# A two-layer transformer on one core: the head's set-up work moved between engines, the end of the program cut in parts, and every slot of the software pipeline set anew

## The chip, the cores and the metric

The kernel runs on one core of a Trainium2 chip. The core has five engines that run their own instruction streams and meet only at semaphores: PE (TensorE, matrix products and transposes, results in the eight banks of PSUM), DVE (VectorE), ACT (ScalarE), POOL (GpSimd) and SP (SyncE, which only issues transfers here). The metric is the device time of one execution in microseconds. Three runs of the kernel before gave 383.49, 383.53 and 386.50 us, a median of 383.53 us.

## The reference, cut to what matters

The reference runs two blocks over x with 8 sequences of 256 tokens and 128 features. Each block adds an attention and a feed-forward part to x, each behind a layer norm:

```
x = x + L0_attn(layernorm(x))    # 16 heads of 8, logits - softplus(alpha_h)*|i-j|, softmax
x = x + tanh(h @ W @ A1 @ A2 + bias)          # h = layernorm(x)
x = x + L1_attn(layernorm(x))    # scores * exp(-0.01*|i-j|), softmax; k, v through a rank-32 latent
x = x + L1_ffn(layernorm(x))     # three +-1 matrices 256->512->512->128, relu between
```

So there are 8 sequences x 2 layers = 16 items of 16 heads, each head a softmax over a matrix of 256x256 scores.

## The kernel before, in words

**Tiling and stages.** An item is one sequence in one layer; items 0 to 7 are layer 0, items 8 to 15 layer 1. The main loop has 16 iterations of 16 slots; a slot `s` of iteration `i` brings head `c = 16*i + s`. A head goes through five stages on four engines: PE computes its scores, four heads at a time, one head in each of banks 0 to 3 (`pe_scores`, L482); DVE adds or multiplies the distance table and takes the row maximum (`dve_max`, L760); the maximum is subtracted; PE transposes the result (`pe_turn`, L504 or L507); ACT takes the exponential (`act_exp`, L946); and PE multiplies four heads with v (`pe_pv`, L519). The turn of a head stands four slots behind its scores, and since it has two banks to turn into, turn c also waits for the exponential of head c-2.

**The kind of shift.** Who subtracts the maximum is read from a table of letters, `SHIFT`, one letter per head of a layer: D is two subtractions on DVE (L776), A two activations on ACT (L954) behind a small POOL instruction, P a small POOL instruction (L1147) and two more products on PE (L496). `SHIFT_LAG` says how many slots later a D or A is done.

**Everything else** rides in the slots of the loop. `SLOTS` gives, for each piece of the work around the heads, the slot at which each engine comes to it, one number for layer 0 and one for layer 1 (which one counts is decided by the iteration's number). `FIRST` replaces these numbers in iteration 0. `SHARED`, `STARTING` and `ENDING` say which PSUM bank each piece uses; banks 0 to 3 are shared with the scores, and a piece of work that enters a bank waits until its last reader is done (`bank_free`). In layer 1 the feed-forward part of an item has the hidden products h0 and h1 (first matrix, 4 products each), h2 and h3 (second matrix, 16 products each, in two halves h2a, h2b, h3a, h3b) and out. ACT evacuates each hidden result twice (`act_hidden`: L937 into the f16 tile fh, L939 into the f32 tile fr), and POOL, or DVE at the end, subtracts the two (`low_hidden`, L1160) to get the low part.

Each engine carries out its instructions in the order in which the loop wrote them. A piece whose input is late holds back all that stands behind it on its engine.

**The head** is the stretch before iteration 0 and in it. DVE zeroes vpad (L1336) and the selection matrix sel (L1337); ACT loads a table set, copies the q weights, loads the set with Ln (L1424), copies xn_t, copies ident16 four times into sel (L1431), loads the set with Exp (L1436), and evacuates k. PE multiplies sel with the f16 parts of q and k (`pe_first`, L457), ACT copies the four results into stack (L974), normalizes item 1 (L1040) and writes six distance tables (`act_adist`, L981). Only then come the scores of heads 0 to 3.

**The end** is written out by hand (`pe_end`, `dve_end`, `act_end`). Item 15's attention output is copied in two halves by DVE (L896) and ACT (L1112) after its last product; then come the transposes, the projection (L564), the residual (L817), the norm (L721, L726, L905, POOL L1324, L910), the hidden products of item 15 one after the other, and the last out (L624, L834, and the store by SP, L1250).

## Time and profile before

| | before |
|---|---|
| median of three runs | 383.53 us |
| the profiled execution, its own time | 385.39 us |
| its span, first to last instruction | 383.6 us |
| mean granted TensorE clock | 0.981 |
| PE busy | 349.2 us (91%), 3664 instructions |
| PE weight loads | 260.0 us (68%) |
| DVE busy | 314.3 us (82%), 1508 instructions |
| ACT busy | 295.7 us (77%), 646 instructions |
| POOL busy | 134.6 us (35%), 354 instructions |

The busy time of an engine counts the time in which at least one of its instructions is under way. The three stretches of the program are read apart below: the head (up to the second group of scores, at 24.40 us), the loop, and the end (from 350 us).

### The profile page before, as it was taken

The numbers are of one execution on the slowest core, as the hardware profiler recorded it, in microseconds if no ns is written. First come the engines' busy times: TensorE is split into PE (matmuls) and PEld (weight loads), VectorE is DVE, ScalarE is ACT, GpSimd is POOL, SyncE is SP. The second block draws the span as 40 slices with busy tenths as digits, with TensorE's granted clock in tenths as the row PEclk, the third lists the DMA queues.
The fourth block names the chain that finished last, engine by engine and source line by source line (L and its number), as shares of the span: only waits on it lengthen the run. The fifth ranks groups of instructions, "written<-read, shape, count | busy, mean of one in ns | idle before, by whom it ended". The sixth has DMA issues, their size and how long they took to land.

```text
span 383.6 us, 11252 instructions
## 1 busy us (share of the span) xinstructions
PE 349.2 (91%) x3664; PEld 260.0 (68%) x3664; DVE 314.3 (82%) x1508; ACT 295.7 (77%) x646; POOL 134.6 (35%) x354
## 2 busy tenths in 40 slices
PE   6588999999999999999999989999899999989774
PEld 4356767777776767676767768777686776767554
DVE  7755899989999999999999998789787888976451
ACT  5956788887879787877878789788987888787552
POOL 2224334343343423343333353444534334333010
PEclk9878999999999999999999999999999999999997
DMA  5103412120213030303212121211122200000000
GB/s 138 54 7 105 104 57 65 48 82 31 74 40 109 18 99 13 100 15 98 75 39 64 48 57 56 58 41 50 37 70 57 59 13 0 17 2 16 2 15 27
DMA packets 29655, 19.79 MB, mean 52 GB/s; under 512 B 4055, under 2 KB 25758, under 8 KB 29598
## 3 DMA queue, kind: packets, MB, share of 16 engines
q1 hardware_dynamic: 29032, 18.82, 16.7%
q8 instruction: 30, 0.49, 0.6%
q10 hardware_dynamic: 566, 0.26, 0.3%
q14 instruction: 27, 0.22, 0.2%
HBM read 10.16 MB, written 8.91 MB: 50 GB/s over the span
## 4 chain that ended last, share of the span: by engine, by line
PE 41%; DVE 5%; issue 4%; ACT 4%; POOL 0%; ACTq 0%; DVEq 0%
PE bank L507 10%; PE bank L545 8%; PE bank L519 8%; PE bank L504 3%; PE bank L482 3%; PE bank L496 2%; PE bank L564 2%; PE bank L624 2%; ACT fr L939 2%; PE bank L556 1%; PE bank L527 1%; DVE scored L760 1%; PE bank L579 1%; DVE rden L800 1%; DVE fh L1160 1%
## 5 line engine op out<-in xcount | busy, mean ns | idle before, releaser
L946 ACT ACTIVATE probs<-bank 128x512 f32<-128x512 f32 x256 | 147.9, 598 | 49.0 <-PE bank L504 24.5
L760 DVE CUSTOM_DVE_ANT_0 scored<-bank,decay 128x256 f32<-128x256 f32 x256 | 93.5, 419 | 18.0 <-PE bank L482 17.1
L760 DVE CUSTOM_DVE_ANT_0 scored<-bank,adist 128x256 f32<-128x256 f32 x256 | 93.2, 418 | 13.6 <-PE bank L482 11.7
L507 PE MATMUL bank<-ident,scored 128*128 128x128 f32 x608 | 90.9, 277 | 2.9 <-ACT probs L946 1.5
L507 PEld LDWEIGHTS bank<-ident,scored 128*128 128x128 f32 x608 | 67.5, 141 | 23.6 <-issue 16.8
L776 DVE TENSOR_SCALAR scored<-scored,mx 128x256 f32<-128x256 f32 x208 | 69.6, 383 | 0.3
L519 PE MATMUL bank<-probs,vpad 128*32 128x256 f32 x1024 | 69.4, 389 | 0.0
L504 PE MATMUL bank<-ident,scored 128*128 128x128 f32 x416 | 63.3, 275 | 0.0
L1147 POOL TENSOR_SCALAR negmax<-mx 128x2 f16<-128x2 f32 x104 | 23.6, 226 | 93.1 <-DVE mx L760 92.4
L504 PEld LDWEIGHTS bank<-ident,scored 128*128 128x128 f32 x416 | 49.5, 143 | 1.3
L954 ACT ACTIVATE scored<-scored,negbias 128x256 f32<-128x256 f32 x96 | 43.8, 515 | 1.1 <-POOL negbias L1147 1.1
L519 PEld LDWEIGHTS bank<-probs,vpad 128*32 128x32 f32 x1024 | 26.9, 109 | 24.9 <-issue 10.5
L760 DVE DVE_READ_ACCUMULATOR2_ANT mx<- 128x1 f32 x512 | 42.4, 83 | 0.0
L496 PE MATMUL bank<-ident,negmax 128*128 128x256 f16 x208 | 40.3, 275 | 2.0 <-ACT probs L946 1.1
L545 PE MATMUL bank<-fh,w_ff 128*128 128x256 f16 x256 | 32.4, 273 | 2.5 <-DVE fh L1160 2.5
L482 PE MATMUL bank<-stack 32*128 32x256 f16 x512 | 25.5, 272 | 8.2 <-issue 4.1
L937 ACT ACTIVATE fh<-bank,s_cols 128x512 f16<-128x512 f32 x32 | 22.2, 692 | 10.3 <-PE bank L545 10.2
L1160 POOL TENSOR_TENSOR fh<-fr,fh 128x512 f16<-128x512 f32 x22 | 26.2, 1191 | 9.2 <-ACT fr L939 9.2
L545 PEld LDWEIGHTS bank<-fh,w_ff 128*128 128x128 f16 x256 | 24.8, 98 | 5.9 <-DVE fh L1160 2.9
L496 PEld LDWEIGHTS bank<-ident,negmax 128*128 128x128 f16 x208 | 16.1, 98 | 18.1 <-issue 14.9
L792 POOL TENSOR_TENSOR parts<-xf,parts 128x512 f16<-128x512 f32 x15 | 17.8, 1185 | 23.3 <-DVE parts L787 23.3
L939 ACT ACTIVATE fr<-bank,s_cols 128x512 f32<-128x512 f32 x32 | 22.2, 693 | 0.0
(180 smaller groups left out, 442.4 us busy)
## 6 DMA issues: line engine op xcount, KB each, us to landing
dqk<-parts SPq DMA_DIRECT2D x120, 64.0 KB, 2.0
stack<-dqk SPq DMA_DIRECT2D x30, 256.0 KB, 2.9
out_dram<-outb SPq DMA_DIRECT2D x8, 128.0 KB, 2.6
x_sb<-in_L_attn_x_dram SPq DMA_DIRECT2D x1, 640.0 KB, 4.6
x_sb<-in_L_attn_x_dram SPq DMA_DIRECT2D x1, 256.0 KB, 4.5
bool_raw<-in_L_ffn_k_dram SPq DMA_DIRECT2D x1, 256.0 KB, 3.4
w_raw<-in_L_attn_qkv_w_dram ACTq DMA_DIRECT2D x1, 128.0 KB, 3.0
x_sb<-in_L_attn_x_dram SPq DMA_DIRECT2D x1, 128.0 KB, 2.8
```

What stands on the lines that cost most here:

```text
L482: mm = pe.matmul(bank[j][:, t * T:(t + 1) * T], stack[rows, par, 0, g, t * P:(t + 1) * P], stack[rows, par, 1, g, :], start=True, stop=Tru ...
L496: pe.matmul(out[:, :].rearrange("p (k t q) -> p t k q", k=QT, t=QT)[:, t, :, :], negmax[:, 2 * r + t:2 * r + t + 1].to_broadcast([P, P]), ...
L504: mm = pe.matmul(dst, src, ident[:, :], start=False, stop=True, is_transpose=True, skip_group_check=True)
L507: mm = pe.transpose(dst, src, ident[:, :])
L519: mm = pe.matmul(ps_acc[32 * j:32 * j + 32, r * T:(r + 1) * T], vpad[:, it % 2, t, HALF * r + 2 * j + e, :], probs[:, (4 * g + j) % RING, ...
L545: mm = pe.matmul(bank[b][:, j * T:(j + 1) * T], w, v, start=(n == 0), stop=(n == len(terms) - 1))
L760: red = dve.tensor_tensor_reduce(scored[:, r, t, :], bank[c % QUAD][:, t * T:(t + 1) * T], tab[:, (1 - t) * P:(1 - t) * P + T], 1.0, NEG_B ...
L776: sh = dve.tensor_scalar(scored[:, r, t, :], scored[:, r, t, :], mx[:, 2 * r + t:2 * r + t + 1], None, ALU.subtract)
L939: act.activation(fr[:, g % 2, :], bank[b][:, :], ACT.Relu, scale=s2_cols[:, l:l + 1]).then_inc(h_sb, 1)
L946: act.activation(probs[:, c % RING, :, :], turn_bank(c)[:, :].rearrange("p (a c) -> p a c", a=2), ACT.Exp).then_inc(probs_ready, 1)
L954: sh = act.activation(scored[:, r, t, :], scored[:, r, t, :], ACT.Identity, bias=negbias[:, 2 * r + t:2 * r + t + 1])
L1160: eng.tensor_tensor(fh[:, l, 1, k:k + 2, :], fr[:, g % 2, :].rearrange("p (k c) -> p k c", k=2), fh[:, l, 0, k:k + 2, :], ALU.subtract).th ...
```

## The change

**Head.** The zeroing of sel goes from DVE to POOL (there as 2048 f16 elements; on DVE it was 1024 words), and the four copies from ident16 into sel from ACT to POOL, behind the reciprocal root of item 0. On ACT the copy of xn_t now stands ahead of the Ln table load, and the Exp table load stands behind the norm of item 1. DVE evacuates and splits q before it computes the slopes and the first two distance tables. Of the four copies into stack, numbers 0 and 2 stay on ACT and numbers 1 and 3 go to DVE (`dve_first`). The product for v waits for its weights by a wait of its own.

**Loop.** `SLOTS`, `FIRST`, `SHIFT`, `SHIFT_LAG` and the bank tables all have new numbers. In layer 0 there are still 8 P, 5 D and 3 A; in layer 1 there were 5 P, 8 D, 3 A and there are now 5 P, 7 D, 4 A.

**End.** Item 15's attention output is gathered in two banks, copied by ACT in two halves (the first one long before the last product) and turned and divided in two halves. Its hidden results go into tiles of their own, fr_last and fh_last: ACT evacuates each once, DVE makes the f16 copy and the difference. The products for h2, h3 and out run by halves and by part, as their inputs come. POOL takes two `low_hidden` from DVE.

```diff
-SHARED = ({"qk": 0, "v": 1, "ft": 7, "f0": 0, "acc": 7, "att": 7, "proj": 7, "xn": 1},
-          {"qk": 7, "v": 0, "ft": 7, "f0": 0, "h3": 0, "h0": 7, "acc": 1,
-           "h1": 1, "out": 7, "att": 7, "proj": 0, "xn": 1, "h2": 7})
+SHARED = ({"qk": 0, "v": 1, "ft": 7, "f0": 0, "acc": 7, "att": 1, "proj": 7, "xn": 0},
+          {"qk": 7, "v": 1, "ft": 7, "f0": 7, "h3": 0, "h0": 7, "acc": 1,
+           "h1": 2, "out": 7, "att": 7, "proj": 0, "xn": 2, "h2": 7})
-SHIFT = ("PPAD" "DPAP" "PPDD" "PAPD", "PDDD" "PDAP" "PADD" "ADPD")
+SHIFT = ("DPAD" "DAPP" "PDPP" "PAPD", "PDDD" "PDDP" "PAPD" "AADA")
...
+    def dve_first(dve, n):
+
+        dve.wait_ge(first_ps, n + 1)
+        half = 2 * (n % 2)
+        dve.tensor_copy(stack[:, 0, n // 2, half:half + 2, :].rearrange("p g t -> p (g t)"),
+                        bank[4 + n][:, :]).then_inc(first_dve, 1)
...
+    def pe_last_deep(pe, g, half, p):
+
+        b = bank_of(f"h{g}", LAST)
+        pe.wait_ge(last_lo if p else last_hi, half + 1)
...
+    def dve_last_hidden(dve, g):
+
+        l, k = g // 2, 2 * (g % 2)
+        dve.wait_ge(last_sb, g + 1)
+        hi, full = fh_last[:, l, 0, k:k + 2, :], fr_last[:, g, :].rearrange("p (k c) -> p k c", k=2)
+        dve.tensor_copy(hi, full).then_inc(last_hi, 1)
+        dve.wait_ge(last_hi, g + 1)
+        dve.tensor_tensor(fh_last[:, l, 1, k:k + 2, :], full, hi, ALU.subtract).then_inc(last_lo, 1)
...
+    def act_last_hidden(act, g):
+
+        act.wait_ge(last_h, g + 1)
+        act.activation(fr_last[:, g, :], bank[bank_of(f"h{g}", LAST)][:, :], ACT.Relu,
+                       scale=s2_cols[:, g // 2:g // 2 + 1]).then_inc(last_sb, 1)
...
         pe_hidden(pe, b, 3, [0, 1])
-        pe_hidden(pe, c, 0, [0, 1])
-        pe_hidden(pe, c, 1, [0, 1])
+        for half in range(2):
+            for p in range(2):
+                for g in (2, 3):
+                    pe_last_deep(pe, g, half, p)
         pe_out(pe, b)
-        pe_hidden(pe, c, 2, [0, 1])
-        pe_hidden(pe, c, 3, [0, 1])
-        pe_out(pe, c)
+        for half in range(2):
+            for p in range(2):
+                pe_last_out(pe, half, p)
...
+        dve.wait_ge(q0_ps, 1)
+        dve.tensor_scalar(xf[:, 0, :], bank[0][:, 0:T], bias0_cols[:, 0:1], SCALE[0], ALU.add, ALU.mult).then_inc(q0_sb, 1)
...
         dve.tensor_tensor(parts[:, 1, 1, :], xf[:, 1, :], parts[:, 0, 1, :], ALU.subtract).then_inc(lo_ready, 1)
+        dve_first(dve, 1)
         dve_ln_mean(dve, 1)
         for n in range(ADIST_EARLY, H - ADIST_ACT):
+            if n == FIRST_COPY:
+                dve_first(dve, 3)
             dve_adist(dve, n)
```

The order of the instructions on ACT in the head, behind the copy of the biases, was this (w_t is a weight, xn_t the normalized input turned, stack the input of the scores, xn the normalized input of item 1; the six distance tables L981 and item 1's xn_t followed):

```order
9 L1424 ACT_TABLE_LOAD
10 L1424 ACTIVATE al_tmp<-al_tmp 128x16
11 L1027 ACTIVATE xn_t<-bank 128x256
12 L1431 ACTIVATE sel<-ident 128x256 x2
13 L1431 ACTIVATE sel<-ident 128x128x2 x2
14 L1436 ACT_TABLE_LOAD
15 L1436 ACTIVATE al_warm<-al_tmp 128x16
16 L1438 ACTIVATE xf<-bank,bias_cols 128x256
17 L1439 ACTIVATE parts<-bank,bias_cols 128x256
18 L1441 ACTIVATE w_t<-bank 128x256
19 L974 ACTIVATE stack<-bank 128x512 x4
20 L1040 ACTIVATE xn<-x_sb,negmean,rstd 128x128 x2
```

And it is now:

```order
9 L1156 ACTIVATE xn_t<-bank 128x256
10 L1593 ACT_TABLE_LOAD
11 L1593 ACTIVATE al_tmp<-al_tmp 128x16
12 L1595 ACTIVATE xf<-bank,bias_cols 128x256
13 L1596 ACTIVATE parts<-bank,bias_cols 128x256
14 L1598 ACTIVATE w_t<-bank 128x256
15 L1103 ACTIVATE stack<-bank 128x512 x2
16 L1169 ACTIVATE xn<-x_sb,negmean,rstd 128x128 x2
17 L1603 ACT_TABLE_LOAD
18 L1603 ACTIVATE al_warm<-al_tmp 128x16
19 L1110 ACTIVATE adist<-toe_abs,al_tmp 128x384 x6
20 L1156 ACTIVATE xn_t<-bank 128x256
```

The xn_t copy stands before the first load, the sel copies are gone, two of the four stack copies are gone, and the second load stands behind xn, ahead of the six distance tables. On PE the same place, from the first scores on, changes from

```order
12 L527 MATMUL bank<-ident,xn 128x128 x2
13 L482 MATMUL bank<-stack 128x256 x8
14 L564 MATMUL bank<-w_t,xn_t 128x128 x2
15 L556 MATMUL bank<-xn_t,w_t 128x256 x2
16 L496 MATMUL bank<-ident,negmax 128x2x128 x2
17 L504 MATMUL bank<-ident,scored 128x128 x4
```

to

```order
12 L505 MATMUL bank<-stack 128x256 x8
13 L592 MATMUL bank<-w_t,xn_t 128x128 x2
14 L553 MATMUL bank<-ident,xn 128x128 x2
15 L584 MATMUL bank<-xn_t,w_t 128x256 x2
16 L530 MATMUL bank<-ident,scored 128x128 x4
```

so that the first scores and the product for v no longer stand behind item 1's transposes, and head 0 is of kind D. In a layer-1 iteration, ACT did the following from slot 11 (the evacuation of h1) to slot 1:

```order
385 L937 ACTIVATE fh<-bank,s_cols 128x512
386 L939 ACTIVATE fr<-bank,s_cols 128x512
387 L946 ACTIVATE probs<-bank 128x512
388 L954 ACTIVATE scored<-scored,negbias 128x256 x2
389 L1017 ACTIVATE att_t<-bank 128x256
390 L946 ACTIVATE probs<-bank 128x512
391 L954 ACTIVATE scored<-scored,negbias 128x256 x2
392 L946 ACTIVATE probs<-bank 128x512 x3
393 L937 ACTIVATE fh<-bank,s_cols 128x512
394 L939 ACTIVATE fr<-bank,s_cols 128x512
395 L1040 ACTIVATE fxn<-x_sb,fnegmean,frstd 128x128 x2
```

and now does

```order
372 L1073 ACTIVATE probs<-bank 128x512
373 L1083 ACTIVATE scored<-scored,negbias 128x256 x2
374 L1146 ACTIVATE att_t<-bank 128x256
375 L1073 ACTIVATE probs<-bank 128x512
376 L1083 ACTIVATE scored<-scored,negbias 128x256 x2
377 L1073 ACTIVATE probs<-bank 128x512 x2
378 L1083 ACTIVATE scored<-scored,negbias 128x256 x2
379 L1073 ACTIVATE probs<-bank 128x512
380 L1083 ACTIVATE scored<-scored,negbias 128x256 x2
381 L1064 ACTIVATE fh<-bank,s_cols 128x512
382 L1066 ACTIVATE fr<-bank,s_cols 128x512
383 L1169 ACTIVATE fxn<-x_sb,fnegmean,frstd 128x128 x2
```

so two more shifts stand between the last exponentials of the item and the evacuation of h2, and the one that stood in slot 8 is gone from there.

## Rows read from the trace of the kernel before

**Rows 1.** Busy time by stretch: us, then PE, PEld, DVE, ACT, POOL; PEclk, DMA
```profile
45.00:200.00 155.00, 149.78 (x1651) 111.56 (x1650) 143.72 (x727) 125.16 (x285) 56.57 (x172) 1.00 0.20 60
225.00:345.00 120.00, 113.74 (x1242) 86.64 (x1240) 98.49 (x472) 100.51 (x210) 49.83 (x101) 1.00 0.14 39
274.00:284.00 10.00, 9.44 (x116) 7.07 (x114) 8.17 (x37) 8.80 (x21) 4.40 (x10) 1.00 0.21 68
350.00:383.60 33.60, 22.45 (x217) 17.32 (x215) 13.61 (x37) 17.12 (x32) 2.59 (x5) 0.93 0.04 13
```

**Rows 2.** Waits of PE, 45 to 200 us, then 225 to 345: total, times, longest
```profile
PE bank L482 <- DVE mx L760: 2.4, 6, 0.9
...
PE bank L482 <- issue: 3.4, 6, 0.6
PE bank L545 <- DVE att L808: 1.5, 6, 0.3
```

**Rows 3.** Timeline of the head: start, us, engine, line, what, [idle before <-releaser]
```profile
3.14 0.91 DVE L1337 MEMSET sel<- 128x1024 uint32 x1 [0.16 <-issue]
...
9.03 1.28 ACT L1436 ACT_TABLE_LOAD   x1
...
11.96 0.28 POOL L1128 TENSOR_TENSOR vpe<-mv,minus 128x2 f32<-128x2 f32 x1 [6.18 <-DVE mv L726]
...
13.28 1.30 ACT L974 ACTIVATE stack<-bank 128x512 f16<-128x512 f32 x2 [0.26 <-PE bank L457]
13.62 0.27 POOL L1134 TENSOR_TENSOR negmean<-vpe,rstd 128x2 f32<-128x2 f32 x1
14.47 0.87 ACT L1040 ACTIVATE xn<-x_sb,negmean,rstd 128x128 f32<-128x128 f32 x2
15.24 3.13 ACT L981 ACTIVATE adist<-toe_abs,al_tmp 128x384 f32<-128x384 f32 x6
...
15.77 0.40 PE L482 MATMUL bank<-stack 32*128 32x256 f16 x8
...
20.54 2.05 PE L556 MATMUL bank<-xn_t,w_t 128*128 128x256 f32 x4 [0.62 <-ACT vpad L993]
```

**Rows 4.** Timeline of a layer-1 iteration: h1, its evacuation, scores; h2's evacuation
```profile
249.93 0.61 PE L545 MATMUL bank<-fx,w_ff 128*128 128x256 f16 x4 [0.26 <-DVE att L808]
...
252.10 0.40 PE L482 MATMUL bank<-stack 32*128 32x256 f16 x8 [0.56 <-issue]
252.32 0.96 ACT L954 ACTIVATE scored<-scored,negbias 128x256 f32<-128x256 f32 x2
...
283.02 0.68 ACT L939 ACTIVATE fr<-bank,s_cols 128x512 f32<-128x512 f32 x1
```

**Rows 5.** The chain that ended last, inside the loop: start, us, what
```profile
284.97 0.87 PE bank L556 x4
```

**Rows 6.** Timeline of the end
```profile
350.54 0.60 ACT L946 ACTIVATE probs<-bank 128x512 f32<-128x512 f32 x1 [0.71 <-PE bank L507]
...
361.99 0.68 PE L564 MATMUL bank<-w_raw,att_t 128*128 128x128 f32 x4 [1.72 <-ACT fr L939]
...
365.39 0.60 DVE L910 TENSOR_SCALAR fxn<-x_sb,fmv,frstd 128x128 f32<-128x128 f32 x2 [0.58 <-POOL frstd L1324]
...
368.73 0.42 DVE L1152 TENSOR_TENSOR fx<-fxn_t,fx 128x256 f16<-128x256 f32 x1
...
370.09 0.69 DVE L1160 TENSOR_TENSOR fh<-fr,fh 128x512 f16<-128x512 f32 x1 [0.94 <-ACT fr L939]
...
373.15 3.67 PE L545 MATMUL bank<-fh,w_ff 128*128 128x256 f16 x32 [1.25 <-DVE fh L1160]
...
377.44 0.68 ACT L939 ACTIVATE fr<-bank,s_cols 128x512 f32<-128x512 f32 x1
...
378.90 1.89 PE L624 MATMUL bank<-w_ff,fh 128*128 128x128 f16 x16 [2.08 <-DVE fh L1160]
380.82 0.48 DVE L834 SCALAR_TENSOR_TENSOR outb<-bank,s_cols,x_sb 128x256 f32<-128x256 f32 x1 [1.98 <-PE bank L624]
```

More of the change, by code:

```diff
@@ L398, in program @@
     last_reader = {}
+    held = set()
     def bank_free(pe, bank_index):
+        assert bank_index not in held
         if bank_index in last_reader:
@@ new lines, in pe_last_out @@
+    def pe_last_out(pe, half, p):
+        b = bank_of("out", LAST)
+        pe.wait_ge(last_lo if p else last_hi, half + 3)
+        if half == 0 and p == 0:
+            bank_free(pe, b)
+        for t in range(QT):
+            for k in (2 * half, 2 * half + 1):
+                mm = pe.matmul(bank[b][:, t * D:(t + 1) * D], fh_last[:, 1, p, k, t * P:(t + 1) * P], w_ff2[:, k, :],
+                               start=(half == 0 and p == 0 and t == 0 and k == 0),
+                               stop=(half == 1 and p == 1 and k == 3), skip_group_check=True)
+        if half == 1 and p == 1:
+            mm.then_inc(h2_ps, 1)
@@ L894, in dve_end @@
         low_input(dve, b)
[L895 to L900 removed]
+        dve_last_attention(dve, 0)
+        dve_last_attention(dve, 1)
         dve_residual(dve, c)
@@ L1441, in _ @@
         act.activation(w0_t[:, 2:4, :].rearrange("p n d -> p (n d)"), bank[3][:, 0:2 * D], ACT.Copy).then_inc(wv_sb, 1)
-        for n in range(4):
+        for n in (0, 2):
             act_first(act, n)
         act_norm_attention(act, 1)
+        act.wait_ge(softplus, 2)
+        act.activation(al_warm[:, :], al_tmp[:, 2, :], ACT.Exp)
         for n in range(H - ADIST_ACT, H):
```

229 lines of the change are left out of this document (161 added, 68 removed), and 6 rows, old and new, of the table FIRST.

## The prediction

> **What bounds the kernel now.** I read busy time by stretch first. In the loop PE is busy 149.8 of 155 us in layer 0 and 113.7 of 120 us in layer 1 [rows 1], DVE follows with 143.7 of 155 (93%) and 98.5 of 120 (82%), ACT with 81% and 84%. The change adds and removes no PE work in the loop: the number of P heads per layer, the only kind that costs PE products, stays at 8 and 5. So the loop can only gain what PE idles. The sum of that is 5.2 us in the first stretch and 6.3 us in the second. The view of PE's waits names part of it [rows 2]: in layer 0 scores wait for DVE's maxima (2.4 us in 6 waits); in layer 1 each iteration has one wait of 0.56 us of scores (3.4 us in 6), one of 0.26 us of h1 (1.5 us in 6) and one of scores behind ACT's fr (1.3 us in 5). In the end PE is busy only 22.5 of 33.6 us [rows 1]: there one chain of dependent steps sets the time, and each step can be followed in the timeline.
>
> **The head.** Sel's zeroing leaves DVE (0.91 us [rows 3]), so item 0's norm can start up to 0.9 us earlier; I take 0.5 for the start of the selection products. On POOL the same tile is 2048 elements instead of 1024 words; by the DVE row that is 1.8 us, and the four copies follow; both lie under ACT's and DVE's work on q, and sel is needed only when q's low part exists, so I cost them at nothing. If POOL were more than about 1 us slower than that, each further microsecond would show in the first scores.
>
> The first scores are the visible gain. They started at 15.77, behind item 1's transposes. Now they wait for the stack copies alone; ACT's third copy ran from 13.28 for 0.65 us (two took 1.30) [rows 3], so the scores can start at 13.9, 1.9 us earlier. But what is behind them gives it back. The next step on PE's path is item 1's product for q and k, at 20.54 before [rows 3]. It needs xn_t of item 1, and that now stands behind more on ACT. DVE computes slopes, two tables, k's low part and a stack copy before it aggregates item 1's statistics. Against before, the slopes and tables delay k's low part by some 0.3 us and the copy adds 0.65 (priced as ACT's copy, the nearest row): POOL's norm starts at about 12.95 instead of 11.96. It takes from 11.96 to 13.89, 1.93 us [rows 3], so it ends at 14.9. Then ACT does xn (0.87), the Exp load, which has been moved here (1.28), six distance tables (3.13) [rows 3]: 20.2. The small exponential and xn_t's copy add about 0.5 (an estimate from xn: two halves of 128 columns take 0.87). The product starts at 20.7 instead of 20.54, and scores of heads 4 to 7 follow it. Head: **+0.2 us**. Bounds: if the delay on DVE does not occur, 1.0 less; if copies on DVE and POOL cost twice their rows, about 1.3 more.
>
> The Trainium skill, page "ScalarE: Activation LUTs", section "What ACT_TABLE_LOAD costs", says that a switch of table set costs a load of 1283 ns plus a drain of about 1380 ns, 2.66 us in all. This trace's row shows the load at 1.28 [rows 3], and ACT's timeline has no further gap around it. By the page the moved load would put the product at 22.1 and the head at +1.6; the sum below goes by the row.
>
> **The loop, layer 1.** In before h1 and the turned attention output shared bank 1, and h1 waited 0.26 us for DVE to finish with it [rows 4]. Now h1 is in bank 2. Its evacuation by ACT holds the bank until just before the next scores, which waited 0.56 us [rows 4]. The evacuation of h0 is moved two slots forward, into the stretch in which ACT waited for PE, so ACT comes free for h1 earlier. The gain per iteration is at least 0 and at most both waits, 0.82 us. I take 0.35: the bank wait with certainty, and little of the second, since ACT can only start when h1 is done. There are 7 full such iterations: **-2.5 us** (0 to -5.7).
>
> Against this stands ACT's queue. Kind A costs 0.96 us on ACT for its two instructions [rows 4]. One more head per item is A, and the A shift of slot 8 is gone while two stand in slots 15 and 0, in front of h2's evacuation. From 274 to 284 us ACT was busy 8.80 of 10 [rows 1], so 1.2 us of the 1.9 fits and at least 0.7 is late. Who waits: the q, k product of slot 2 goes into bank 7, where h2 lies. h2's fr ended at 283.70 [rows 4], the product began at 284.97 [rows 5]: 1.27 us of cover. A delay of 0.7 is hidden, the full 1.9 would cost 0.65 per iteration. I cost it at nothing.
>
> **The loop, layer 0.** Same work, other slots. DVE is at 93% and PE at 97%; whatever the order gains is at most the waits that [rows 2] shows, 2.4 us, and a bad order can lose as much. I take **0** (+-2.4).
>
> **The end.** At its start ACT now does head 255's shift before head 252's exponential, which was at 350.54 [rows 6]: up to 0.96 and its wait later, say 1.2. On the other side the projection, at 361.99, had waited 1.72 us for ACT's fr of another item [rows 6], which held its bank; it has a bank of its own now, and half the attention output is copied and turned before the last heads are through. I let these cancel: the normalized item 15 is ready at 366.0 as before (365.39 + 0.60 [rows 6]). Bounds: 1 earlier, 1.2 later.
>
> From 366.0: before, the difference that h0 and h1 wait for ran at 368.73 for 0.42, and ACT had evacuated item 14's h2 (two of 0.68 [rows 6]) ahead of item 15's copies. These two stand behind now: 368.73 - 1.36 + 0.42 = 367.8. The products of the f16 part run under the difference, and four more take 0.4 at the rate of 32 in 3.67: h0 and h1 exist at about 368.1. ACT evacuates each once, 0.68 instead of two activations [rows 6]: 368.8 and 369.4. PE meanwhile has item 14's h3, half of the 3.67 that 32 such products take [rows 6], until 370.0. Then the 32 deep products of item 15 start, instead of at 373.15 [rows 6], where they waited for DVE's last difference. DVE's four steps for h0 and h1 (an f16 copy, between the 0.48 of L834 and the 0.69 of L1160, I take 0.45; and 0.69 [rows 6]; twice: 2.3 us from 368.8) end at 371.1, ahead of the products that need them. So these end at 370.0 + 3.67 = 373.7, 3.1 us earlier than 376.8. Item 14's out takes 0.9 more on PE; ACT gives h3 by 374.4; DVE's last four steps run from 373.9 to 376.2, the last quarter of out is done at 376.6. On DVE item 14's output stands in front of item 15's: 0.48 each [rows 6], 377.2. The store takes as long as it did, from 381.30 to 383.6, 2.3 us: 379.5. The end: 379.5 - 383.6 = **-4.1 us** (-5.1 to -2.9).
>
> **Sum.** +0.2 - 2.5 + 0 - 4.1 = -6.4 us. The profiled execution took 385.39 us with a span of 383.6; one like it would take 379.0. The median of the runs shown is 383.53, 1.86 us less than the profiled one; on it the sum gives **377.1 us**.
>
> **The rivals.**
> 1. *The loop does not pay.* Head and end as above, the new slots neutral or a little worse: 383.53 + 0.2 - 4.1 = 379.6, and with the full 0.65 per iteration in slot 2 (7 times 4.6) 384.2. For it: a table of slots is a periodic schedule in which a gain at one slot often appears as a wait in another, and PE has only 3 to 5% left. Chance 0.26.
> 2. *The loop pays twice.* Both waits of layer 1 go (-5.7) and layer 0's too (-2.4): 371.5. For it: in layer 1 ACT's order is built around just these waits; against it: DVE at 93% in layer 0. Chance 0.14.
> 3. *Slower.* ACT's crowd at slots 15 to 1. If nothing hides the two shifts (1.9 us) in each of 7 iterations, since the exponential of head 13 behind them also releases the turn of head 15, the loop loses 13.4: 383.53 - 3.9 + 13.4 = 393. It is slower by over 1% once the stall passes 1.1 us per iteration, (3.8 + 3.9)/7. Against it: the 1.2 us of room on ACT and the 1.27 us of cover. Chance 0.08.
> 4. *The moved load costs as the page has it.* As a mechanism of this kernel: ACT is idle behind the load for a further 1.4 us before the six tables, and all of it reaches the q, k product: 378.5. Against it: no such gap in the trace. Chance 0.02.
> 5. *The forecast*, 374 to 379.7. Chance 0.50.
>
> **How the numbers follow.** A measurement of this kernel can tell about 1%, 3.8 us, from no change. Faster than 379.7: the forecast (nearly all of 0.50), rival 2 (0.14), rival 4 (0.02) and a small part of rival 1: 0.68. Within 1%: the rest of rival 1: 0.24. Slower: 0.08. The range from 372.0 to 383.0 leaves out the lower half of rival 2, the upper part of rival 1 and rival 3, together 0.2; the forecast's own range is 374 to 380.
>
> **What would show it.** In the new profile: the first scores start near 13.9 us and the q, k product of item 1 near 20.7; if the latter comes at 19 or before, the head's step is wrong. In a layer-1 iteration h1 has no wait on DVE's att, and PE's busy share from 225 to 345 us rises above 94.8%; if ACT's fr of h2 is what the slot-2 product waits for, rival 1 or 3 is running. In the end the 32 deep products start 3 us nearer to fxn than the 7.2 us of before (373.15 - 366.0), and from the end of fxn to the end of the span it is 13.5 us instead of 17.6. If that last stretch is not below 15 us, the largest term of the sum is wrong. The forecast fails if the loop, from 45 to 345 us, is not shorter.

## The result and the profile after

The changed kernel takes **372.89 us** (median of 4 runs, 372.18 to 373.27), the kernel before in the same session 383.75 us (383.49 to 386.5). The ratio is 0.970, 95% interval 0.965 to 0.975: 3.0% faster, 10.9 us. The prediction said 377.1 us, 6.4 us less than before, with a range of 372.0 to 383.0. The direction is right and the time lies inside the range, but 1.1 us below the forecast's own span (374 to 380): some 4.5 us of gain came from something that the sum had not. That the range still held it is not owed to its reasons, as the parts below show.

The profiled execution of the changed kernel took 372.58 us with a span of 370.6 us. Busy time by stretch (the columns are those of [rows 1]); the loop is shorter, so the stretches are 10 us earlier:

```profile
45.00:195.00 150.00, 147.96 (x1653) 111.64 (x1646) 140.50 (x724) 123.49 (x282) 57.19 (x172) 1.00 0.21 62
215.00:335.00 120.00, 114.74 (x1268) 88.68 (x1267) 96.30 (x471) 102.39 (x220) 51.55 (x110) 1.00 0.14 41
350.00:370.60 20.60, 14.73 (x134) 11.90 (x132) 10.37 (x25) 8.04 (x15) 2.84 (x3) 0.88 0.07 20
```

PE's busy share in layer 0 rose from 96.6% to 98.6%, in layer 1 from 94.8% to 95.6%. What is left of its waits, 45 to 190 us and 215 to 335 us (total us, times, longest), against [rows 2]:

```profile
PE bank L505 <- DVE mx L852: 1.1, 4, 0.4
PE bank L530 <- ACT probs L1073: 0.6, 2, 0.3
PE bank L519 <- ACT probs L1073: 0.3, 1, 0.3
```
```profile
PE bank L505 <- ACT fr L1066: 5.0, 10, 0.7
```

In layer 0 scores still wait for DVE's maxima, but for less than half as long. In layer 1 h1's wait for att is gone, and nearly all that remains is scores waiting behind ACT's fr.

To see where time comes from I use one mark through the whole program: the start of the score products. "It 1" is the first score group of iteration 1 (the head ends there), "it 8" the first of iteration 8 (layer 0's loop ends), "last" the last group of the program. All are read from the timeline of PE, in us:

| kernel | it 1 | it 8 | last | span | it 1 to 8 | it 8 to last | last to end |
|---|---|---|---|---|---|---|---|
| before | 42.44 | 175.08 | 344.99 | 383.6 | 132.64 | 169.91 | 38.6 |
| after | 39.43 | 167.92 | 336.22 | 370.6 | 128.49 | 168.30 | 34.4 |
| difference | -3.01 | -7.16 | -8.77 | -13.0 | **-4.15** | **-1.61** | **-4.2** |

The head, the two layers and the end gave 3.0, 4.2, 1.6 and 4.2 us. The prediction had a head 0.2 us longer and gains of 0, 2.5 and 4.1. The end's total agrees, layer 1 was forecast too large, and layer 0 and the head are what was missed. The table's sum is 13.0 and the medians differ by 10.9. Most of the difference is that the profiled execution of before took 1.6 us more than the median of its session and that of after 0.3 us less than its own; the first experiment shows what such a difference is made of. About 1.7 of the 3.0 and 4.2 us for head and end belong to it.

### The profile page after: what moved, and what is told of

Read it like the earlier page. It is cut to its first block, busy times and chain, and to the rows that moved or that the text cites. A ratio compares the mean times of both kernels' runs of the same rounds, so it can differ in the third digit from the quotient of the medians.

```text
span 370.6 us, 11255 instructions
## 1 busy us (share of the span) xinstructions
PE 345.8 (93%) x3664; PEld 260.5 (70%) x3664; DVE 308.3 (83%) x1495; ACT 294.7 (80%) x653; POOL 140.9 (38%) x369
## 4 chain that ended last, share of the span: by engine, by line
PE 78%; ACT 10%; DVE 5%; issue 5%; DMA 1%; POOL 1%; ACTq 0%; DVEq 0%; POOLq 0%
PE bank L530 19%; PE bank L545 15%; PE bank L527 9%; PE bank L571 6%; PE bank L505 5%; PE bank L519 5%; PE bank L584 4%; PE bank L592 4%; ACT probs L1073 2%; PE bank L553 2%; ACT fr L1066 2%; PE bank L609 2%; DVE scored L852 2%; ACT fh L1064 1%; PE bank L654 1%
## 5 line engine op out<-in xcount | busy, mean ns | idle before, releaser
L530 PE MATMUL bank<-ident,scored 128*128 128x128 f32 x608 | 89.1, 279 | 1.6 <-ACT probs L1073 1.6
L530 PEld LDWEIGHTS bank<-ident,scored 128*128 128x128 f32 x608 | 66.8, 141 | 27.0 <-issue 20.4
L884 DVE TENSOR_SCALAR scored<-scored,mx 128x256 f32<-128x256 f32 x192 | 62.1, 368 | 0.9
L527 PE MATMUL bank<-ident,scored 128*128 128x128 f32 x416 | 62.4, 272 | 0.0
L1083 ACT ACTIVATE scored<-scored,negbias 128x256 f32<-128x256 f32 x112 | 50.8, 511 | 0.0
L527 PEld LDWEIGHTS bank<-ident,scored 128*128 128x128 f32 x416 | 48.7, 141 | 1.2
L1313 POOL TENSOR_TENSOR fh<-fr,fh 128x512 f16<-128x512 f32 x24 | 28.0, 1165 | 17.5 <-ACT fr L1066 17.5
L1300 POOL TENSOR_SCALAR negbias<-mx 128x2 f32<-128x2 f32 x56 | 12.4, 221 | 57.8 <-DVE mx L852 57.2
L571 PE MATMUL bank<-fh,w_ff 128*128 128x256 f16 x224 | 30.2, 281 | 2.2 <-DVE fh L1313 2.2
L571 PEld LDWEIGHTS bank<-fh,w_ff 128*128 128x128 f16 x224 | 22.3, 100 | 5.3 <-DVE fh L1313 2.4
L505 PEld LDWEIGHTS bank<-stack 32*128 32x128 f16 x512 | 8.0, 92 | 18.8 <-issue 13.7
L1064 ACT ACTIVATE fh<-bank,s_cols 128x512 f16<-128x512 f32 x28 | 19.3, 690 | 1.4 <-PE bank L571 1.4
```

What stands on the lines that cost most here:

```text
L505: mm = pe.matmul(bank[j][:, t * T:(t + 1) * T], stack[rows, par, 0, g, t * P:(t + 1) * P], stack[rows, par, 1, g, :], start=True, stop=Tru ...
L527: mm = pe.matmul(dst, src, ident[:, :], start=False, stop=True, is_transpose=True, skip_group_check=True)
L530: mm = pe.transpose(dst, src, ident[:, :])
L571: mm = pe.matmul(bank[b][:, j * T:(j + 1) * T], w, v, start=(n == 0), stop=(n == len(terms) - 1))
L884: sh = dve.tensor_scalar(scored[:, r, t, :], scored[:, r, t, :], mx[:, 2 * r + t:2 * r + t + 1], None, ALU.subtract)
L1083: sh = act.activation(scored[:, r, t, :], scored[:, r, t, :], ACT.Identity, bias=negbias[:, 2 * r + t:2 * r + t + 1])
```

## The experiments

### The kernel before once more

No edit.

> The kernel before, unchanged, profiled once more. The profile on which the prediction rests took 385.39 us where the median of before is 383.5 to 383.8, and it shows TensorE at half its clock twice in the head: about 17.5 to 23.9 us and about 31.1 to 34.8 us. The changed kernel shows only the first. Theory A (the second stretch at half clock is a matter of the single execution): the new profile lacks it, the scores of heads 12 to 15 start near 36.5 instead of 38.27, and its own time is near 383.5. Theory B (the order of work in iteration 0 of the kernel before brings it about): it is there again and the time is near 385.

Measured: 383.83 us, span 382.0. Its marks are 41.66, 174.29 and 344.26: layer 0 takes 132.63 us and layer 1 169.97 us, within 0.06 of the first profile. The loop repeats to a few hundredths; head and end don't. Here is one stretch of the head, 32 to 34 us, in the first profile of before, and below it in this one (the clock is the last column but two):

```profile
32.00:34.00 2.00, 2.00 (x15) 1.48 (x8) 0.96 (x6) 0.04 (x1) 1.49 (x6) 0.50 0.36 105
```
```profile
32.00:34.00 2.00, 2.00 (x17) 1.82 (x16) 0.97 (x6) 1.23 (x3) 1.48 (x6) 1.00 0.16 43
```

In the first, PE was granted 0.50, that is 1.2 of 2.4 GHz, and 16 products with the probabilities took 1.90 us there against 1.07 in the loop; just ahead of it the scores at 30.30 had waited 0.71 us (0.56 in the second, at 30.31). In the second the clock was full. The third quarter of item 0 (30.3 us to the next scores) took 7.97 us in the one and 6.34 in the other. A part of that is made good in the next quarter, and iteration 1 begins 0.8 us apart.

The end is 0.9 us shorter too, and again it is the clock. The 16 products of the last out took 1.89 us in the first profile ([rows 6], 378.90), where the clock was at 0.50 from about 378.9 us on, and in this one, at full clock:

```profile
378.18 1.07 PE L624 MATMUL bank<-w_ff,fh 128*128 128x128 f16 x16 [2.09 <-DVE fh L1160]
```

So differences in head and end of this size between two profiles can be the clock alone, and only the loop can be read to a tenth.

### The change in parts, added one after another

Three kernels start from before and take over more and more. The first has the new end (functions for the last item, `ENDING`) and nothing else; the second also layer 1's numbers, the third also layer 0's. The head stays old in all three.

```diff
-ENDING = {15: {"acc": 0, "att": 1, "proj": 2, "ft": 3, "h0": 4, "h1": 6, "h2": 2, "h3": 0, "out": 1},
+ENDING = {15: {"att": 2, "proj": 7, "ft": 4, "h0": 7, "h1": 1, "h2": 2, "h3": 0, "out": 4},
...
+            for p in range(2):
+                for g in (2, 3):
+                    pe_last_deep(pe, g, half, p)
```

> The kernel before with the new end alone (the gathered halves, the tiles of their own for the last item, the new order of the last products and the new banks of the last three items); head and all slots as before. Theory of the prediction: 4.1 us less, all of it behind the last scores, so 379.5 us. The comparison of the two traces says 4.2 us. Rival (the new end gains only because the new slots deliver to it in another order): less than 2.5 us.

Measured: 379.82 us (379.58 to 380.19), ratio 0.987 (0.983 to 0.991): 5.0 us. Span 377.8; the stretch from the last scores to the end is 32.6 us instead of 38.6, or instead of 37.7 in the second profile of before, which fits the 5.0. The rival (less than 2.5 us) is out: the new end pays with the old slots too.

```diff
-          {"qk": 7, "v": 0, "ft": 7, "f0": 0, "h3": 0, "h0": 7, "acc": 1,
-           "h1": 1, "out": 7, "att": 7, "proj": 0, "xn": 1, "h2": 7})
+          {"qk": 7, "v": 1, "ft": 7, "f0": 7, "h3": 0, "h0": 7, "acc": 1,
+           "h1": 2, "out": 7, "att": 7, "proj": 0, "xn": 2, "h2": 7})
...
-SHIFT = ("PPAD" "DPAP" "PPDD" "PAPD", "PDDD" "PDAP" "PADD" "ADPD")
+SHIFT = ("PPAD" "DPAP" "PPDD" "PAPD", "PDDD" "PDDP" "PAPD" "AADA")
```

> As end_only, and in addition the new slots, banks, kinds of shift and lags of layer 1. The prediction's theory: a further 2.5 us (0.35 per iteration), 377.0 us. From the comparison of the two traces, layer 1's eight iterations are 1.6 us shorter in sum: 377.9 us. Rival (layer 1's numbers pay nothing, the difference comes from what layer 0 hands over): within 0.5 us of end_only.

Measured: 378.94 us (376.99 to 379.39), ratio 0.983 (0.979 to 0.988). Layer 1 from mark to mark: 168.12 us instead of 169.92, 1.8 less; by the ratios it is 1.4, with an uncertainty as large as that. The trace is what measures it.

```diff
-SHIFT = ("PPAD" "DPAP" "PPDD" "PAPD", "PDDD" "PDDP" "PAPD" "AADA")
+SHIFT = ("DPAD" "DAPP" "PDPP" "PAPD", "PDDD" "PDDP" "PAPD" "AADA")
```
(with layer 0's slots, lags and banks)

> As end_and_layer1, and in addition the new slots, banks, kinds and lags of layer 0; only the head and iteration 0's own table are the old ones. The prediction held layer 0 at 0: 377 us or as end_and_layer1. The comparison of the traces puts 4.0 us on layer 0's iterations 1 to 7: 373.9 us. If the missing gain sits in the head instead, this one stays above 376 us.

Measured: 373.47 us (372.67 to 374.12), ratio 0.970 (0.967 to 0.974). Layer 0's numbers alone bring 5.1 us by the ratios and 4.16 us from mark to mark (132.64 to 128.48). Nothing of the new head is in this kernel, and its ratio is that of the changed kernel. The traces give the head 1.7 us (41.15 against 39.43 at iteration 1), the ratios don't tell it from nothing.

### Layer 0 put back, whole and by halves

The changed kernel once more, and then with all of layer 0's numbers old:

> The changed kernel, unchanged, on the same chip as the three below. Theory A: 372.9 us again, with single executions about 1 us apart, since the half-clock stretches differ from one to the next. Against end_and_both_layers (373.5 us), which differs in the head alone, the prediction's head of +0.2 says 373.3 or the same; the traces say 1.7 us less, 371.8.

Measured: 372.6 us (372.12 to 373.09), ratio 0.970 (0.968 to 0.972); marks 39.57, 168.05, 336.35.

```diff
-SHIFT = ("DPAD" "DAPP" "PDPP" "PAPD", "PDDD" "PDDP" "PAPD" "AADA")
+SHIFT = ("PPAD" "DPAP" "PPDD" "PAPD", "PDDD" "PDDP" "PAPD" "AADA")
```
(with layer 0's slots, lags and banks)

> The changed kernel with layer 0's slots, banks, kinds of shift and lags as they were before; head, iteration 0's table, layer 1 and end are the new ones. If layer 0 is worth the 4.0 us that lie between the two traces, it takes 376.9 us. The prediction held this at 0: 372.9. If layer 0's numbers pay only together with the old head, something between.

Measured: 378.04 us (377.76 to 378.28), ratio 0.984 (0.982 to 0.986): 5.4 us are lost again. Layer 0 from iteration 1 to 8 takes 134.14 us instead of 128.49. Added last or taken away first, layer 0 is worth 4.2 to 5.6 us by the marks. The difference of 1.5 us is all in iteration 1, which takes 20.14 us here and 18.63 before: behind the new head and iteration 0's new table the old numbers meet waits that before hasn't, such as 0.81 us for DVE's maxima at 51.21. Without that misfit layer 0's numbers are worth 4.2 us. This is the largest single piece beside the end, where the prediction had nothing.

Iterations 1 to 7 became shorter by 0.22, 0.39, 0.53, 0.53, 0.85, 0.81 and 0.82 us. To see how, the last quarter of iteration 6 on PE, from one score group to the next. Before (start, us, row; idle before in brackets):

```profile
151.45 0.40 PE L482 MATMUL bank<-stack 32*128 32x256 f16 x8
...
153.45 0.60 PE L507 MATMUL bank<-ident,scored 128*128 128x128 f32 x4
153.94 0.41 PE L527 MATMUL bank<-ident,xn 128*128 128x128 f32 x2
154.39 0.63 PE L507 MATMUL bank<-ident,scored 128*128 128x128 f32 x4
154.88 0.38 PE L496 MATMUL bank<-ident,negmax 128*128 128x256 f16 x2
...
156.04 0.40 PE L482 MATMUL bank<-stack 32*128 32x256 f16 x8 [0.35 <-DVE mx L760]
```

And after:

```profile
145.53 0.40 PE L505 MATMUL bank<-stack 32*128 32x256 f16 x8
...
147.36 0.38 PE L519 MATMUL bank<-ident,negmax 128*128 128x256 f16 x2
147.57 0.60 PE L527 MATMUL bank<-ident,scored 128*128 128x128 f32 x4
148.01 0.38 PE L553 MATMUL bank<-ident,xn 128*128 128x128 f32 x2
148.30 0.38 PE L519 MATMUL bank<-ident,negmax 128*128 128x256 f16 x2
...
149.70 0.40 PE L505 MATMUL bank<-stack 32*128 32x256 f16 x8
```

A head of kind P has a negmax row in front of its turn and takes PE 0.65 us (147.36 to 148.01); a head of another kind has only the turn, 0.44 to 0.49 us (153.45 to 153.94). Before, this quarter had two P and two others; after, it has three P and one other, more PE work, and yet lasts 4.17 us instead of 4.59. Two pauses are gone: the 0.35 us for which the next scores waited for DVE's maxima (DVE has a shift less to do here), and one that no bracket names. The two transposes of xn were followed by the next turn after 0.45 us (153.94 to 154.39) and are so now after 0.29 (148.01 to 148.30). A turn needs the exponential of the head two before it, because there are two banks to turn into; when the turn comes too early, PE stands for a tenth or two, and the view of waits doesn't list that. ACT's rows, before and after, bear it out here:

```profile
153.65 0.60 ACT L946 ACTIVATE probs<-bank 128x512 f32<-128x512 f32 x1 [1.35 <-PE bank L504]
```
```profile
147.56 0.60 ACT L1073 ACTIVATE probs<-bank 128x512 f32<-128x512 f32 x1 [1.35 <-PE bank L530]
```

This is the exponential of head 9, the first that the quarter turns. It ends at 154.25 and 148.16, and in both kernels the turn of head 11 begins 0.14 us behind that end (154.39 and 148.30). Head 9 was of kind P and is now of kind D, so its turn has no product in front of it, and its exponential starts 2.03 us behind the scores instead of 2.20.

The place that the third P head comes from is the first quarter. There before had two P heads and lasted 5.20 us (137.01 to 142.21); after has one and lasts 4.98 (131.48 to 136.46), which is what one negmax product costs. So a P head was taken from a quarter in which PE had no pause, where it cost its full 0.22 us, and put into one where PE paused anyway, where it cost nothing. The count per layer is the same, as the prediction said; the cost is not. The four quarters of iteration 6 were 5.20, 4.45, 4.79 and 4.59 and are 4.98, 4.46, 4.61 and 4.17: 19.03 against 18.22 us. The other iterations were not read row by row.

Is it the letters (which engine shifts which head) or the slots (when the small steps run)? First the letters and lags put back:

```diff
-SHIFT = ("DPAD" "DAPP" "PDPP" "PAPD", "PDDD" "PDDP" "PAPD" "AADA")
+SHIFT = ("PPAD" "DPAP" "PPDD" "PAPD", "PDDD" "PDDP" "PAPD" "AADA")
-SHIFT_LAG = ("2321223113311222", "3121122213211231")
+SHIFT_LAG = ("2311211323211233", "3121122213211231")
```

> The changed kernel with one thing of layer 0 put back: the letters that say which engine shifts each head's turned bias (PPAD DPAP PPDD PAPD instead of DPAD DAPP PDPP PAPD) and their lags. The slots and the banks of layer 0 stay new. With all of layer 0's tables old the kernel took 378.0 us, with all new 372.6 to 372.9, so 5.3 us are to be divided. Theory A, the letters: the old order puts two heads in a row that wait for the exps of two heads earlier (heads 10 and 11 on VectorE's shifts), and the gaps between their turns and the score group's wait on VectorE's maxima are the 5 us; then 376.5 to 378.5 us here. Theory B, the slots: moving VectorE's and TensorE's small steps within the iteration is what brings it; then 372.5 to 374 us. Theory C, each suits the other: this mixture is worse than either whole set, above 378.5 us.

Measured: 376.88 us (376.7 to 378.49), ratio 0.980 (0.975 to 0.984). Iteration 1 to 8 takes 133.32 us, 4.8 more than after. The quarters of iteration 6 are 5.19, 4.46, 4.79 and 4.34: the first, the third and a part of the last are those of before again. Iterations 2 to 4 of this kernel take 18.96, 19.29 and 19.55 us, longer than before (18.61, 18.75 and 19.00), and the whole is 0.7 us longer than layer 0 of before: here the old letters do not suit the new slots. The waits from 45 to 190 us are back as well:

```profile
PE bank L505 <- DVE mx L852: 2.8, 6, 0.9
```

Then the other half, layer 0's `SLOTS` and banks (`SHARED[0]`) put back and the letters new:

```diff
-SHARED = ({"qk": 0, "v": 1, "ft": 7, "f0": 0, "acc": 7, "att": 1, "proj": 7, "xn": 0},
+SHARED = ({"qk": 0, "v": 1, "ft": 7, "f0": 0, "acc": 7, "att": 7, "proj": 7, "xn": 1},
...
-    "qk": (2, 2), "v": (2, 2), "xn": (14, 14), "acc": (8, 10), "att": (10, 12), "proj": (12, 13), "ft": (4, 4),
+    "qk": (2, 2), "v": (3, 2), "xn": (14, 14), "acc": (7, 10), "att": (10, 12), "proj": (12, 13), "ft": (3, 4),
```

> The reverse of the run before: the changed kernel with layer 0's slots and bank numbers put back, its letters and lags new. Theory A (letters): 372.5 to 374 us. Theory B (slots): 376.5 to 378.5 us. Theory C (each suits the other): above 378.5 us.

Measured: 374.62 us (373.6 to 375.71), ratio 0.973 (0.969 to 0.977); iteration 1 to 8 takes 130.86 us, 2.4 more than after. It lies between the two theories' bands. Its iteration 6 has quarters of 4.98, 4.58, 4.61 and 4.17 us, all but those of the changed kernel; in other iterations one is longer (the last of iteration 3 takes 4.65 us, in the changed kernel 4.17). The waits add up to more than twice those of after:

```profile
PE bank L488 <- DVE mx L835: 2.5, 6, 0.7
```

So the letters are the larger part (4.8 us when undone, by the marks; 3.8 by the ratios) and the slots the smaller one (2.4 and 1.2). In iterations 5 to 7 the letters are worth nearly 0.6 us each and the slots 0.1. The two don't add up, since both undone cost 5.65, not 7.2; a part of each, mostly in iterations 2 to 4, is the price of a mixture.

### Layer 1 by its two parts

The prediction put its certain gain on h1's bank. Put back:

```diff
-           "h1": 2, "out": 7, "att": 7, "proj": 0, "xn": 2, "h2": 7})
+           "h1": 1, "out": 7, "att": 7, "proj": 0, "xn": 2, "h2": 7})
```

> The changed kernel with one number of layer 1 put back: h1 goes to bank 1 again instead of bank 2, so that it waits once more until VectorE has taken the attention's product out of that bank (0.26 us in each iteration of the kernel before). The prediction's step counted that wait as gained in 7 iterations: by it this run is 1.8 us slower than the changed kernel, 374.4 to 374.8 us. The rival, which the changed kernel's trace suggests: the next score group waits 0.74 us behind a residual step on ScalarE that stands later than h1, so that time saved at h1 is waited out there; then the run is within 0.5 us of the changed kernel, 372.4 to 373.2 us.

Measured: 373.44 us (372.69 to 374.73), ratio 0.970 (0.966 to 0.973). The time is nearer to the rival's band, but its interval is as wide as the question. The marks decide: it 8 to last takes 169.71 us, 1.41 more than after, and the difference is 0.21 to 0.29 us in each of the six iterations 10 to 15, the only ones with an h1. The rows of one iteration, here with h1 in bank 1 (h1, its second evacuation by ACT, the next scores):

```profile
242.42 0.61 PE L569 MATMUL bank<-fx,w_ff 128*128 128x256 f16 x4 [0.26 <-DVE att L914]
...
243.66 0.68 ACT L1064 ACTIVATE fr<-bank,s_cols 128x512 f32<-128x512 f32 x1
...
244.44 0.40 PE L503 MATMUL bank<-stack 32*128 32x256 f16 x8 [0.53 <-issue]
```

and in the changed kernel, with h1 in bank 2:

```profile
241.58 0.60 PE L571 MATMUL bank<-fx,w_ff 128*128 128x256 f16 x4
...
242.85 0.69 ACT L1066 ACTIVATE fr<-bank,s_cols 128x512 f32<-128x512 f32 x1
...
243.79 0.40 PE L505 MATMUL bank<-stack 32*128 32x256 f16 x8 [0.74 <-ACT fr L1066]
```

The quarter that holds h1 is 5.85 us long in the first and 5.63 in the second, from scores to scores. H1 starts 0.41 us earlier in it (241.58 - 238.16 against 242.42 - 238.59): the named 0.26 and a pause ahead of it that has no name. But the scores come 2.21 us behind h1 instead of 2.02, so about half is given back and 0.22 us remain. The scores write banks 0 to 3, and h1 stands in bank 1 or 2: they need h1's second evacuation to be over. It ends at 244.34 in the one, with the scores at 244.44, and at 243.54 in the other, with the scores 0.25 behind; why the last step is 0.15 longer I can't show. Some of the time saved at h1 is thus waited out behind ACT's fr, as the rival says, but 1.4 us are there all the same, which the timed runs can't resolve. The prediction's 1.8 took the wait of 0.26 seven times; [rows 2] lists it six times, 1.5 us, and nearly all of that is gained.

Then the letters and lags of layer 1:

```diff
-SHIFT = ("DPAD" "DAPP" "PDPP" "PAPD", "PDDD" "PDDP" "PAPD" "AADA")
+SHIFT = ("DPAD" "DAPP" "PDPP" "PAPD", "PDDD" "PDAP" "PADD" "ADPD")
```

> The changed kernel with layer 1's letters and lags put back (PDDD PDAP PADD ADPD instead of PDDD PDDP PAPD AADA), slots and banks of layer 1 new. The new order gives ScalarE two of its three shifts behind one another at heads 12 and 13 and one at head 15, close to the residual step for which the next scores wait 0.74 us. Theory A, ScalarE's shifts near the turn of the iteration are what ate the gain of layer 1: the old letters bring 0.3 to 0.5 us an iteration, 369 to 371 us. Theory B, the letters and the slots were set together, and the old letters wait elsewhere (the first shifts on ScalarE at head 6 and 9): within 1 us of the changed kernel or slower, 372 to 376 us.

Measured: 376.73 us (375.0 to 377.52), ratio 0.978 (0.974 to 0.981). It 8 to last takes 173.01 us, 4.7 more than after (the ratios give 3 us) and 3.1 more than before. ScalarE's crowded shifts were not what ate layer 1's gain; without them it is worse. The scores' wait behind fr is unchanged and a new one has come, a turn that waits for a shift on ACT (waits from 215 to 335 us, then the row in the timeline):

```profile
PE bank L505 <- ACT fr L1066: 5.0, 10, 0.7
PE bank L530 <- ACT scored L1083: 1.8, 4, 0.5
```
```profile
242.06 0.66 PE L530 MATMUL bank<-ident,scored 128*128 128x128 f32 x4 [0.45 <-ACT scored L1083]
```

The old letters have this shift on ACT with the old slots too, and before it didn't wait. Letters and slots are one schedule: old letters with new slots are 3.1 us worse than the old pair and 4.7 worse than the new one.

### The half clock in the head and in the end

The changed kernel still has two stretches at half clock, one at each place where PE idles for long: in the head from about 17.5 to 24.3 us, in the end from about 355.4 to 358.8. (From 369 us on it is at half again, where PE has no work left.) Busy time by stretch, the clock in the last column but two:

```profile
20.00:22.00 2.00, 1.09 (x3) 0.95 (x4) 1.04 (x6) 1.85 (x6) 0.03 (x1) 0.50 0.00 0
22.00:24.00 2.00, 2.00 (x9) 1.54 (x7) 0.14 (x1) 1.00 (x3) 0.00 (x0) 0.50 0.00 0
```
```profile
356.60:358.60 2.00, 2.00 (x12) 1.40 (x10) 0.82 (x2) 0.66 (x2) 0.00 (x0) 0.50 0.00 0
```

Dummy transposes keep PE busy there. They go into banks that are free, and nothing reads them; the computation is the same. First in the head only:

```diff
                 pe_v(pe, i)
+                if i == 0:
+                    pe_warm(pe, 14, 6)
...
                     pe_xn_t(pe, 1)
+                    pe_warm(pe, 20, 6)
```

> The changed kernel with 14 transposes of the identity into a free bank behind item 0's product for v and 20 behind item 1's transposes, in PE's two waits of the head. Theory (PE's idling brings the half clock of 16.6 to 24.2 us): the clock stays at full speed, item 1's product takes 0.9 instead of 2.04 us, the second scores start at about 22.8 instead of 24.50, and the time falls by 1 to 1.7 us. Rival (the half clock is set by something else, or ACT sets the pace here anyway): no change, or 0.3 us slower.

Measured: 370.7 us (369.71 to 370.88), ratio 0.964 (0.962 to 0.966): 1.9 us less than the changed kernel in the same session. The second score group starts at 22.95 instead of 24.50. Then 16 more behind the last projection:

```diff
         pe_proj(pe, c)
+        pe_warm(pe, 16, 0)
         pe_hidden(pe, b, 2, [0])
```

> As warm_head, and 16 more such transposes behind item 15's projection, where PE waits 2.2 us for DVE. In the changed kernel's profile the clock is at half from about 355.9 to 359 us; end_and_layer1 did without it in one execution and was 1.4 us shorter in this stretch. Theory: a further 1 to 1.5 us less than warm_head, and single executions closer together. Rival (the transposes delay the h2 products that wait behind them): 0 to 0.3 us slower than warm_head.

Measured: **369.63 us** (369.45 to 369.74), ratio 0.962 (0.960 to 0.964), the fastest kernel here, 3.0 us less than the changed kernel. Its mean clock is 1.000. The same three places:

```profile
20.00:22.00 2.00, 1.35 (x8) 1.23 (x9) 0.79 (x4) 1.81 (x7) 0.00 (x0) 1.00 0.03 8
22.00:24.00 2.00, 1.88 (x21) 0.99 (x19) 1.21 (x6) 2.00 (x6) 0.83 (x1) 1.00 0.00 0
```
```profile
17.64 2.35 PE L468 MATMUL bank<-ident 128*128 128x128 f32 x20
20.65 1.10 PE L584 MATMUL bank<-xn_t,w_t 128*128 128x256 f32 x4 [0.67 <-ACT xn_t L1160]
...
22.69 0.40 PE L505 MATMUL bank<-stack 32*128 32x256 f16 x8
```

The product for q and k takes 1.10 us instead of 2.04, and the group behind it starts 1.8 us earlier. In the end, from the end of fxn to the end of the span, it is 13.3 us instead of 14.6. What the transposes in the end add is not settled: the profile of the kernel with those in the head alone shows full clock in the end as well, and 33.2 us from the last scores, as with both. The median is 1.1 us lower and the runs lie closer together (0.3 us instead of 1.2); that would fit an end that is sometimes at half clock. The mean clocks on record fit it as well: in the profiled execution of the kernel with the head's transposes alone it is 1.000 with a span of 367.8 us, in its other three 0.993 to 0.995 with spans of 368.7 to 369.0; with both sets of transposes all four lie at 0.998 to 1.000 and 367.5 to 367.8. So those three had some microseconds at half clock. That they lay in the end is not shown, since none of them was profiled.

## Why the prediction was right, and where it was not

**The head, right up to the second scores.** The rows named by the prediction, in the changed kernel (those of before are [rows 3]):

```profile
1.76 1.80 POOL L1455 MEMSET sel<- 128x2048 f16 x1
...
13.30 0.28 POOL L1281 TENSOR_TENSOR vpe<-mv,minus 128x2 f32<-128x2 f32 x1 [6.07 <-DVE mv L818]
...
15.05 0.88 ACT L1169 ACTIVATE xn<-x_sb,negmean,rstd 128x128 f32<-128x128 f32 x2 [1.12 <-POOL negmean L1287]
15.95 1.28 ACT L1603 ACT_TABLE_LOAD   x1
17.24 0.22 ACT L1603 ACTIVATE al_warm<-al_tmp 128x16 f32<-128x16 f32 x1
17.37 3.13 ACT L1110 ACTIVATE adist<-toe_abs,al_tmp 128x384 f32<-128x384 f32 x6
```
```profile
14.08 0.40 PE L505 MATMUL bank<-stack 32*128 32x256 f16 x8
...
20.91 2.04 PE L584 MATMUL bank<-xn_t,w_t 128*128 128x256 f32 x4 [2.60 <-ACT xn_t L1156]
```

Sel's zeroing takes the 1.8 us estimated. The first scores are at 14.08 (forecast 13.9), POOL's norm ends at 15.0 (14.9), the product for q and k is at 20.91 (20.7). The second scores stand at 24.50, 0.1 later than before: the 1.7 us won at the first scores are given back behind xn_t, as the step said. The load costs what its row says: the next instruction of ACT starts 0.01 us behind it, so the further 1.38 us of the Trainium skill's page "ScalarE: Activation LUTs" (What ACT_TABLE_LOAD costs) don't appear, and rival 4 is out.

What the step left out lies behind its last number. From there to iteration 1, before took 18.04 us and after 14.93. Of these 3.1 us, 0.6 belong to the one execution of before (its repeated profile has 17.46), 0.5 come with layer 0's numbers (16.99 with the old head and both layers new), and about 2 with the new head and the moved steps of `FIRST`. These 2 us are seen in traces only. 0.9 of them lie in the first quarter behind the second scores (5.54 against 4.60 us), where the mean clock is 0.82 in the one and 1.00 in the other. The other 1.1 lie in the two quarters behind it (11.45 against 10.33), at full clock in both profiles, so they are no matter of the clock; a wait of 0.6 us for POOL's negmax and one of 0.2 for DVE's maxima are gone there. Which moved step brings them was not tried.

**The end, right in sum.** The forecast was -4.1, the marks say -4.2 and the part alone 5.0 by its ratio. That the first two agree is luck: two errors cancel, as shown below. Besides, both are measured from a profile whose 17.6 us from fxn to the end contain 0.9 us of half clock in the last out; the second profile of before has 16.7, and against that one the end gives 3.4 us. The rows that answer to [rows 6]:

```profile
355.44 0.60 DVE L1037 TENSOR_SCALAR fxn<-x_sb,fmv,frstd 128x128 f32<-128x128 f32 x2 [0.58 <-POOL frstd L1488]
...
358.35 1.24 PE L737 MATMUL bank<-fx,w_ff 128*128 128x256 f16 x8
...
361.18 3.66 PE L751 MATMUL bank<-fh_last,w_ff 128*128 128x256 f16 x32
...
367.29 1.06 DVE L942 SCALAR_TENSOR_TENSOR outb<-bank,s_cols,x_sb 128x256 f32<-128x256 f32 x2
```

The 32 deep products start 5.1 us behind fxn (361.18 - 356.04), where 7.2 was before and 4.0 was forecast. From fxn to the end of the span it is 14.6 us, inside the bound of 15 and above the 13.5 forecast. The missing 1.1 us is the half clock, the first error. The kernel with the end alone had full clock in this stretch, here two windows around its fxn:

```profile
363.00:365.00 2.00, 1.48 (x12) 1.11 (x13) 0.93 (x3) 0.00 (x0) 0.88 (x1) 1.00 0.00 0
365.00:367.00 2.00, 2.00 (x21) 1.64 (x19) 0.82 (x2) 1.01 (x3) 0.00 (x0) 1.00 0.02 4
```

and there fxn ended at 364.51 and the span at 377.8: 13.3 us. The chain of steps was thus added up to 0.2 us. The second, which balances it, is the term set to zero, the start of the end: from the last scores to the end of fxn it took 21.0 us before and takes 19.8 now (19.3 with the end alone). The bound there was 1 us earlier, and it is 1.2 to 1.7. So the projection's bank and the early half of the attention should outweigh the shift on ACT that I had set against them; neither was tried by itself.

**Layer 1, right in kind, a little large.** -2.5 was forecast and -1.6 measured, -1.8 with the end alone around it. The term for h1's wait (0.26 in each of 7) gave 1.4 of its 1.8, mostly because there are six such iterations and not seven. The 0.09 per iteration expected from the scores' wait is not there: the scores wait for h1's own evacuation, and that wait is 0.74 us now where it was 0.56. ACT's two neighbouring shifts cost nothing that the waits name, so the cover of 1.27 us held and rival 3 had no ground: the product of slot 2 has no wait in the changed kernel.

**Layer 0, wrong.** The failed step is "whatever the order gains is at most the waits that [rows 2] shows, 2.4 us", and the term 0 that came of it. The gain is 4.15 us, outside its own bound. The bound was wrong by the kernel's own page: PE idled 5.2 of 155 us there [rows 1], which the prediction itself had worked out, and the wait it used is 2.4 of them. Another 1.1 us stood in the same view of before:

```profile
PE bank L507 <- ACT probs L946: 0.8, 2, 0.4
PE bank L496 <- ACT probs L946: 0.3, 1, 0.3
```

The last 1.7 has no name; the one pause of this kind that was read stood ahead of a turn. After the change PE idles 2.0 of 150 us. Per iteration of 18.9 and 18.4 us this is 0.64 and 0.25 us idle, so idle time gives 0.4 of the 0.6 us gained; the rest is in the rows that count as busy, such as the two xn transposes that last 0.45 us before and 0.29 after, where a pause lies under the modelled end of a product. The second fault is the sentence that equal counts of P leave PE's work the same and the order can therefore do little: moving one P head out of a full quarter into one with a pause is exactly a gain at equal counts, and both strings of letters stood in the diff.

That the measured time is inside the stated range is luck too: the range reached down to 372.0 for rival 2's sake, and nothing in the sum leads to 372.9. Rival 2 (the loop pays twice, 371.5 us) is nearer to the time than the forecast, 1.4 us off instead of 4.2, but not by its mechanism: it had 5.7 us in layer 1 and 2.4 in layer 0, where 1.6 and 4.2 were found.

## What to carry to other kernels

When an engine is over 95% busy and the order is what changes, bound the gain by its whole idle time in the stretch, not by the waits that the trace names; here the wait taken for the bound was less than half of it. Even that is a guide and no strict bound: of the 4.15 us gained only some 2.7 were idle time in the profile, the rest lay in rows that count as busy. In a periodic schedule ask of each optional step (here the shift as a product on PE) in which quarter it stands: the same step costs its full length where the engine runs through and nothing where the engine pauses. Test numbers that were set together as a whole: in layer 1 half of such a set was 4.7 us worse than all of it, and 3.1 us worse than none, by the marks.

## What the runs showed of the hardware

The clock of PE cost more than expected in a kernel whose mean clock is 0.98. Idle times of PE of 1.7 and 2.6 us in the head were followed or crossed by 6.8 us at 0.50, one of 2.2 us in the end by 3.4 us, and 34 transposes of no use in the head, 16 in the end, took 3.0 us off the kernel. The same idle time did not always have that effect: the end with a pause of 2.19 us ran at full clock in one kernel and the end with 2.20 us at half clock in another, and of two profiles of the kernel before one has a second dip in the head and one has not. The loop, in contrast, repeats closely from kernel to kernel where its numbers are the same: layer 0 to 0.05 us in 130, layer 1 to 0.06 us in 170 with the same head and 0.18 (168.12 against 168.30) with the other, so that marks in the trace resolve effects of 1 us that three to five timed rounds leave open.
